# First expert weights of a routed feed-forward block: scaled beforehand by ScalarE and fetched per tile by DMA, in place of a VectorE pick per tile

## The reference

```python
def _ffn(xn, rw, W1, W2):
    ms = jnp.mean(xn * xn, axis=-1, keepdims=True)
    h = xn * jax.lax.rsqrt(ms + RMS_EPS) * rw          # rw: one weight per channel and expert
    return jax.nn.silu(h @ W1) @ W2                    # W1 128x256, W2 256x128
gates = jax.nn.softmax(xf @ router_w, axis=-1)
top_v, top_i = jax.lax.top_k(gates, TOP_K)             # 2 of 14
masked = jnp.zeros_like(gates).at[jnp.arange(N)[:, None], top_i].set(top_v)
masked = masked / (masked.sum(axis=-1, keepdims=True) + EPS)
routed = jax.vmap(lambda rw_, W1_, W2_: _ffn(xf, rw_, W1_, W2_))(rms_w, w1, w2)
routed_out = jnp.einsum('end,ne->nd', routed, masked)
shared = jax.vmap(lambda rw_, W1_, W2_: _ffn(xf, rw_, W1_, W2_))(rms_w_s, w1_s, w2_s).sum(0)
x = _layernorm(x + routed_out + shared)                # x: the mixer's normalised output
```

## Time and profile before

| | |
|---|---|
| runs | 769.55 us median of 3 (768.49 to 770.16) |
| span of the profiled execution | 769.2 us; the page gives no other time for it |
| busy share of the span | TensorE 85%, VectorE 77%, GpSimd 65%, ScalarE 58% |
| instructions of VectorE | 1744, of them 141 picks |
| DMA | 70.8 MB, mean 92 GB/s |

### The profile page before, as it was taken

How to read it: one execution, slowest core, us unless ns; L and a number is a source line. 1 busy time by engine, 2 the same in 40 slices (tenths; PEclk the granted TensorE clock), 3 DMA queues, 4 the chain that set the end, 5 groups by cost and what they waited for, 6 DMA issues and landing times.

```text
span 769.2 us, 14716 instructions
## 1 busy us (share of the span) xinstructions
PE 651.3 (85%) x4299; PEld 554.7 (72%) x4299; DVE 596.1 (77%) x1744; ACT 444.7 (58%) x1225; POOL 501.3 (65%) x545
## 2 busy tenths in 40 slices
PE   5987798999999999999999997965988878767830
PEld 4765576788888888888888886854987768656720
DVE  4999999999999999999999864427447343698875
ACT  4885688867877876787787543411223111346445
POOL 1144565887797897888888776556655656566561
PEclk9999999999999999999999998878889889997865
DMA  8541111211221121111111055114222236536126
GB/s 305 193 138 42 43 43 41 64 57 55 62 64 62 60 62 50 63 64 60 59 50 62 22 167 192 45 55 101 80 80 77 76 80 172 168 100 205 60 80 218
DMA packets 62638, 70.76 MB, mean 92 GB/s; under 512 B 10335, under 2 KB 45285, under 8 KB 62304
## 3 DMA queue, kind: packets, MB, share of 16 engines
q1 hardware_dynamic: 41568, 47.70, 19.6%
q0 software_dynamic: 8608, 16.87, 6.5%
q10 hardware_dynamic: 12384, 5.26, 2.9%
HBM read 48.55 MB, written 23.01 MB: 93 GB/s over the span
## 4 chain that ended last, share of the span: by engine, by line
PE 60%; DVE 13%; issue 12%; ACT 7%; another core or an unknown queue 4%; ACTq 2%; DMA 1%; DVEq 0%; SPq 0%
PE bank L745 7%; PE bank L817 6%; PE bank L826 6%; PE bank L884 6%; PE bank L770 5%; PE bank L800 5%; DVE xbcT_area L1155 3%; PE bank L881 3%; PE bank L871 3%; PE bank L833 3%; PE bank L785 3%; PE bank L888 2%; DVE decay_area L1163 2%; ACT x L933 2%
## 5 line engine op out<-in xcount | busy, mean ns | idle before, releaser
L623 POOL DMA_INDIRECT returned<-xT,slots_in x141 | 142.1, 1008 | 107.6 <-DVE xT L1453 67.3
L669 POOL DMA_INDIRECT dispatched<-rows,row_u x128 | 143.7, 1123 | 33.9 <-issue 31.8
L745 PE MATMUL bank<-xT 128*128 128x128 f32 x564 | 92.0, 316 | 43.4 <-issue 24.9
L1155 DVE SCALAR_TENSOR_TENSOR xbcT_area<-raw,conv_w,xbcT_area 128x512 f32<-128x512 f32 x162 | 123.9, 766 | 2.9 <-ACT xbcT_area L999 2.9
L745 PEld LDWEIGHTS bank<-xT 128*128 128x128 f32 x564 | 82.7, 226 | 50.7 <-issue 42.4
L944 ACT ACTIVATE raw<-bank 128x512 f32<-128x512 f32 (+1 forms) x71 | 39.8, 590 | 126.9 <-remote 61.5
L661 POOL TENSOR_TENSOR state_kept<-state,whole 128x256 f32<-128x256 f32 x56 | 72.1, 1288 | 59.0 <-DVE state L1181 49.1
L1453 DVE COPY xT<-bank 128x512 f32<-128x512 f32 (+1 forms) x36 | 24.3, 676 | 90.5 <-remote 72.8
L770 PE MATMUL bank<-xbcT_area,raw 128*128 x564 | 83.4, 308 | 4.7 <-issue 4.6
L1163 DVE TENSOR_TENSOR_SCAN decay_area<-decay_area,ident_heads 128x512 f32<-128x512 f32 x64 | 85.0, 1329 | 0.0
L770 PEld LDWEIGHTS bank<-xbcT_area,raw 128*128 128x128 f32 x564 | 79.6, 224 | 7.0 <-issue 7.0
(11 more groups left out here) (228 smaller groups left out, 1497.0 us busy)
## 6 DMA issues: line engine op xcount, KB each, us to landing
decay_area<-decay_rows SPq DMA_DIRECT2D x64, 256.0 KB
slots_in<-dispatched ACTq DMA_DIRECT2D x77, 64.5 KB
hid<-returned SPq DMA_DIRECT2D x18, 256.0 KB
slots_in<-dispatched SPq DMA_DIRECT2D x64, 64.5 KB
xT<-xT_dram SPq DMA_DIRECT2D x8, 512.0 KB, 7.9
x<-x_dram SPq DMA_DIRECT2D x8, 512.0 KB, 7.8
out_dram<-x SPq DMA_DIRECT2D x16, 256.0 KB
xT<-returned SPq DMA_DIRECT2D x14, 256.0 KB
```

The costliest lines, as they stand in the source:

```text
L623: e.indirect_dma_start(returned, bass.IndirectOffsetOnAxis(ap=slots_in[sb_][:, n, D:ROW].bitcast(U32), axis=0), slots_out[b][:, n * P:(n + ...
L669: e.indirect_dma_start(dispatched, bass.IndirectOffsetOnAxis(ap=row_u[t % 2][:, m:m + 1], axis=0), rows[t % 3][:, k, c4, :], None).then_in ...
L745: mm = e.matmul(bank[:, off:off + P], w1_now[b][:, k * P:(k + 1) * P], slotsT[gr % len(slotsT)][:, n % 4 * P:(n % 4 + 1) * P], start=True, ...
L1155: e.scalar_tensor_tensor(o, r[:, n:n + W], conv_w[:, k, TAPS - 1 - n:TAPS - n], o, ALU.mult, ALU.add).then_inc(S["conv"])
```

## The change

- The 14 routed experts' first weights have an SBUF area of their own (`w1_area`, 14 KB in a partition). SyncE loads them there in step 22 of the mixer; ScalarE multiplies each expert's 128x256 by its norm weights in steps 24 to 37, in place, one in each step; SyncE waits for the 14 and writes the 1792 KB to a DRAM tensor `w1_ready` in step 40.
- SyncE's queue fetches for each tile its expert's 128x256 (128 KB) from `w1_ready`, with the expert's number from a register, into a ring of 3 groups of 4 (`w1_ring`, in the area of the mixer's decays). The fetch for group gr waits until the first matmuls of group gr-3 are done. It stands behind the slot load of the same group and ahead of `pick`.
- VectorE's picks, their register loads and the 8 buffers are gone; TensorE's first matmuls wait for the fetch and read the ring.
- SyncE's `pick` stands one group nearer (`PICKS_BEHIND = 6` in place of the 7 of the slot buffers), and 11 of the picks are in the loop over groups, not 10.
- The 14 KB come in part from `dynamic_dma_scratch_size=2048`: the area in each partition that holds the descriptors of GpSimd's DMAs is 2048 bytes, not the usual 16384.

```diff
     ROUTED_AT = [NC + 2, *range(NC + 3, NC + 13, 2), *range(NC + 13, LAST)]
+    W1_FROM = 24
+    PICKS_BEHIND = 6
...
+    w1_ready = nc.dram_tensor("w1_ready", [P, NR, HB * P], F32, kind="Internal").ap()
...
-        w1_routed = decay_area[:].rearrange("p n h i -> p (n h i)")[:, 0:NR * HB * P].rearrange("p (e f) -> p e f", e=NR)
+        w1_area = sb("w1_area", [P, NR * HB * P])
+        w1_routed = w1_area[:].rearrange("p (e f) -> p e f", e=NR)
+        w1_ring = decay_area[:].rearrange("p n h i -> p (n h i)")[:, 0:3 * 4 * HB * P].rearrange("p (b n f) -> p b n f", b=3, n=4)
...
+                if c == W1_FROM - 2:
+                    e.dma_start(w1_routed, w1_v[:, 0:NR]).then_inc(S["w1r_loaded"], 16)
+                if c == W1_FROM + NR + 2:
+                    on.wait_ge("w1r_scaled", NR)
+                    e.dma_start(w1_ready, w1_routed).then_inc(S["w1r_stored"], 16)
...
+            def fetch_w1(gr, experts):
+
+                b = gr % 3
+                if gr >= 3:
+                    on.wait_ge("routed_hidden", 2 * (gr - 3) + 2)
+                for n in range(len(slot_tiles(gr))):
+                    e.dma_start(w1_ring[:, b, n, :], w1_ready[:, bass.ds(experts[4 * (gr % 2) + n], 1), :].rearrange("p o f -> p (o f)")).then_inc(S[f"w1_in{b}"], 16)
+
-            picks_beside = min(NM, GROUPS - len(slots_in) - LAST_A)
+            picks_beside = min(NM, GROUPS - PICKS_BEHIND - LAST_A)
...
-                if gr == 1:
-                    on.wait_ge("mix", NC)
-                    e.dma_start(w1_routed, w1_v[:, 0:NR]).then_inc(S["w1r_loaded"], 16)
+                if gr == 0:
+                    on.wait_ge("w1r_stored", 16)
...
                     load_slots(e, gr, first_rows)
-
-                m = gr - len(slots_in) - LAST_A
+                if gr == 0:
+                    on.wait_ge("mix", NC)
+                if gr % 2 == 0:
+                    w1_experts = experts_of(on, ET.SP, gr)
+                fetch_w1(gr, w1_experts)
+
+                m = gr - PICKS_BEHIND - LAST_A
...
-                    on.wait_ge("w1_picked", n + 1)
+                    gr = n // 4
+                    on.wait_ge(f"w1_in{gr % 3}", 16 * tiles_upto(gr, 3))
...
-                        mm = e.matmul(bank[:, off:off + P], w1_now[b][:, k * P:(k + 1) * P], slotsT[gr % len(slotsT)][:, n % 4 * P:(n % 4 + 1) * P], start=True, stop=True)
+                        mm = e.matmul(bank[:, off:off + P], w1_ring[:, gr % 3, n % 4, k * P:(k + 1) * P], slotsT[gr % len(slotsT)][:, n % 4 * P:(n % 4 + 1) * P], start=True, stop=True)
...
+                if at(i, W1_FROM, NR):
+                    n = i - W1_FROM
+                    on.wait_ge("w1r_loaded", 16)
+                    on.wait_ge("rms_w_loaded", 16)
+                    e.activation(w1_routed[:, n, :], w1_routed[:, n, :], ACT.Copy, scale=rms_w[:, n:n + 1]).then_inc(S["w1r_scaled"])
...
-            def pick_w1(gr):
-                if gr % 2 == 0:
-                    experts[:] = experts_of(on, ET.DVE, gr)
-                on.wait_ge("w1r_loaded", 16)
-                for n in slot_tiles(gr):
-                    was = n - len(w1_now)
-                    if was >= 0:
-                        on.wait_ge("routed_hidden", was // 2 + 1)
-                    e.tensor_scalar(w1_now[n % len(w1_now)], w1_routed[:, bass.ds(experts[n % 8], 1), :].rearrange("p o f -> p (o f)"), rms_w[:, bass.ds(experts[n % 8], 1)], None, ALU.mult).then_inc(S["w1_picked"])
...
-    nc = bacc.Bacc("TRN2", target_bir_lowering=False, num_devices=1)
+    nc = bacc.Bacc("TRN2", target_bir_lowering=False, num_devices=1, dynamic_dma_scratch_size=2048)
```

More of the change, by code:

```diff
@@ L33 @@
     "mix", "y_carried", "y_sum", "skip_diag", "gated", "residual", "ln_stats", "shift",
-    "logits", "top", "hot", "rows_taken", "shared_added", "w1_scaled", "early_total", "early_table", "table", "slots_turned", "w1_picked",
+    "logits", "top", "hot", "rows_taken", "shared_added", "w1_scaled", "early_total", "early_table", "table", "slots_turned",
     "routed_out", "gate", "routed_added", "last_rstd",
     "rate", "dt_exp", "chunk_decays", "step_decay", "rows_copied", "xbc_raw", "xbc_silu", "z_silu", "xdt", "g_squares", "bt",
-    "gT_copied", "x1", "x2", "xn", "xnT_copied", "hidden_silu", "routed_silu", "gate_exp", "second_scaled",
+    "w1r_scaled", "gT_copied", "x1", "x2", "xn", "xnT_copied", "hidden_silu", "routed_silu", "gate_exp", "second_scaled",
     "dt_raw", "chunk_sums", "rows_turned", "xbc", "z", "token_major", "gram", "state_add", "y_out", "gT",
@@ L342, in mamba_moe @@
         slotsT = [carve(W) for _ in range(3)]
-        w1_now = [carve(HB * P) for _ in range(8)]
         gexp = carve(NC * NR).rearrange("p (c r) -> p c r", c=NC)
@@ L394, in mamba_moe @@
             [f"{n}_loaded" for n, _, _ in small_params] + [f"xT{b}_loaded" for b in range(NB)]
-            + [f"x{b}_loaded" for b in range(NB)] + ["w_in_loaded", "w1_loaded", "w2_loaded", "w1r_loaded", "w2r_loaded",
+            + [f"x{b}_loaded" for b in range(NB)] + ["w_in_loaded", "w1_loaded", "w2_loaded", "w1r_loaded", "w1r_stored", "w2r_loaded",
                "filler_region", "filled", "dispatched0", "dispatched1", "stored", "decay_rows"]
@@ L398, in mamba_moe @@
             + [f"slots_in{b}" for b in range(len(slots_in))] + [f"returned{b}" for b in range(len(slots_out))]
-            + [f"picked{b}" for b in range(len(picked))])
+            + [f"w1_in{b}" for b in range(3)] + [f"picked{b}" for b in range(len(picked))])
         S = {n: ctx.enter_context(nc.semaphore(n)) for n in (*COMPUTE_SEMAPHORES, *dma_semaphores)}
@@ L739, in routed_hidden @@
                 for n in range(2 * n2, min(2 * n2 + 2, SLOT_TILES)):
-                    gr, b = n // 4, n % len(w1_now)
-                    on.wait_ge("w1_picked", n + 1)
+                    gr = n // 4
+                    on.wait_ge(f"w1_in{gr % 3}", 16 * tiles_upto(gr, 3))
                     on.wait_ge("slots_turned", gr + 1)
@@ L1442, in next_group @@
                     turned(gr + 2)
-                    pick_w1(gr + 2)
             def routed_group(gr):
@@ L1609, in vector_program @@
                         turned(gr)
-                        pick_w1(gr)
                 elif n is not None and n >= 2:
```

1 line of the change is left out of this document (removed).

## The result

| | runs | median us | range |
|---|---|---|---|
| before | 7 | 769.89 | 768.14 to 771.67 |
| changed | 7 | 774.75 | 772.21 to 778.20 |

The ratio is 1.0062 (95% interval 1.0039 to 1.0086): 0.6% slower. I had forecast 766.6 us, faster. The value lies in the range of 755 to 780 us, the sign is wrong.

A forecast was written before the change was run, and what follows sets the result against it. Bound: in the middle GpSimd's scatters plus a slow stretch (TensorE gaps, VectorE idle until just after the scatters), in the last part VectorE. Span 769.2 -3.1 -1.8 +1 +1 = 766.3, median 0.35 above: 766.6 us; range 755 to 780.

The forecast's parts named there:

- (c): Beginning of the routed part: without eight picks GpSimd's wait for row numbers goes, 1.8 us gained, bounds 0 and 4.
- (e): SyncE's queue in series: fills behind group 9's fetch delay group 10's transpose, 1 us lost, bounds 0 and 6.
- (a): Last part without VectorE's picks: slow stretches return and GpSimd becomes the limit, 3.1 us gained, bounds 13.2 or nothing.
- (b): Middle without VectorE's picks: they lie beside scatters and don't hold GpSimd up, 0, at most 5.6 us gained.
- the rival of the gain taken back: Slow stretches return and slow VectorE's small token steps, last part gains 0, beginning offset by fills: 769 us, chance 0.17.
- VectorE set free: Rival: in the last part no slow stretches return, a pair takes 11.3 us: 756.5 us in all, chance 0.12.
- (d): ScalarE's 14 scalings in the mixer: 0.38 us each, hidden while it idles for TensorE, 0; 5.3 us without that cover.
- (f): SyncE's token-row picks spread behind fetches: fit with 1.5 us to spare, 0; otherwise 1 us for each of 14 units.
- (g): Extra DMA traffic of 18 MB over 290 us: 1 us lost, bounds 0 to 1.8.
- the 32 us that the prediction gives beside its sum: Estimate from the skill's HBM latency rule for added traffic: up to 1.8 us per pair, not used in the sum.
- (h): Smaller descriptor area for GpSimd's scatters: two in flight, so 0; 36 us if each scatter waits for room.

The follow-up runs named there:

- no_picks_2: Kernel before without VectorE's picks, first matmuls reading fixed unscaled weights in place, with slow stretches: 765.63 us, ratio 1.0016.
- set 3: Set of runs with slow stretches; the changed kernel run again there took 769.34 us, ratio 1.0039 to the kernel before.
- pause_and_fills: Changed kernel with eight unread VectorE multiplications ahead of the row numbers and the fills ahead of group 9's fetch, with slow stretches: 765.41 us, ratio 0.9989.
- unread: Kernel before, picks kept, with 2048-byte area, 141 fetches nobody reads, fills ahead, token-row picks six groups behind; with slow stretches: 774.62 us, ratio 1.0125.
- near_rows: Kernel before with only SyncE's picks of token rows six groups behind in place of seven, with slow stretches: 764.91 us, ratio 0.9984.
- set 2: Set of runs without slow stretches; the changed kernel run again there took 715.30 us, ratio 0.9957 to the kernel before.
- no_picks: Kernel before without VectorE's picks, first matmuls reading fixed unscaled weights in place, without slow stretches: 715.05 us, ratio 0.9938.
- area_only: Kernel before with only GpSimd's descriptor area at 2048 bytes, without slow stretches: 717.22 us, ratio 0.998.
- behind_7: Changed kernel with SyncE's picks of token rows seven groups behind in place of six, with slow stretches: 787.23 us, ratio 1.0239.
- fills_ahead_3: Changed kernel with the fourteen fills moved ahead of group 9's fetch, with slow stretches: 768.51 us, ratio 1.0019.
- picks_on_act: Kernel before with its 141 picks given to ScalarE in place of VectorE, no fetches, with slow stretches: 775.28 us, ratio 1.0142.
- scalings_only: Kernel before with 2048-byte area plus the mixer's weight load, fourteen ScalarE scalings and store, results unread, with slow stretches: 765.26 us, ratio 0.997.
- pause_kept_2: Changed kernel with eight unread VectorE multiplications put back ahead of the row numbers, with slow stretches: 766.43 us, ratio 1.0028.

## Why the prediction was wrong

The step that failed is (c): I counted the pause ahead of the row numbers as 1.8 us to gain, and it was what kept a step of TensorE out of the slow stretch. With it (e) was mis-sized. With slow stretches the picks' end alone, (a), (b) and (c) together, was forecast at 4.9 us gained; `no_picks_2` measured 1.0016 (0.9996 to 1.0036), nothing. In substance that is the rival of the gain taken back, which I had at 0.17.

- **(a) picks, last part: right in size, in part by luck.** Forecast 3.1 us gained, with slow stretches returning; traced 4.8 for the same piece (75.39 to 70.61), and 3.6 in set 3 between scatters. The pairs of the changed kernel's last part are 13.1 to 13.9 us, and `no_picks_2` shows the round of 13.0 us that I took from the middle. But the stretches returned only in part: the changed kernel's copies wait 6.2 us in four such waits there, and `pause_and_fills` has 1.5 us in one and still needs 71.2 us. Nor is all of it the picks': `unread` keeps them and needs 72.4 us, and `near_rows` needs 74.6. In the runs without slow stretches the other bound nearly came true: in the profile of the changed kernel in set 2 the 11 groups take 64.9 us, 11.8 for a pair (groups 31 to 33: 672.62 to 684.05, 11.4), with 11.3 forecast for VectorE set free. How much of that is the picks is open: `no_picks` needs 70.0 us there and `area_only` 71.3.
- **(b) picks, middle: right**, 0. The scatters' mean is 1005 ns for 1008. The rule that VectorE's two-port instructions hold GpSimd up (the Trainium skill, "SBUF — State Buffer", Who interferes with whom) doesn't show in these scatters.
- **(c) beginning: wrong.** Forecast 1.8 gained. The wait went, and 0.2 us were lost to group 4. All twelve profiles with slow stretches split by the pause, whatever else their kernels have:

  | | TensorE idle before the router step that the changed kernel has at 481.11, us | 97th scatter to group 4, us |
  |---|---|---|
  | no pause: changed, changed in set 3, `behind_7`, `fills_ahead_3`, `no_picks_2`, `picks_on_act` | 6.35, 3.38, 7.91, 7.91, 7.85, 4.20 | 87.4, 86.1, 88.6, 88.8, 88.6, 90.0 |
  | pause: before, `near_rows`, `scalings_only`, `pause_kept_2`, `pause_and_fills`, `unread` | none shown in any | 87.2, 84.2, 83.4, 84.5, 82.2, 89.2 |

  `unread` is late for the reason given with it. The kernel before is 3 to 4 us over its near relatives in this stage, in an execution that was slow among its runs, and that hid the loss in the first comparison. `pause_and_fills` (0.9989, up to 1.0007) against `fills_ahead_3` (1.0019, from 0.9997), from two sets, prices it at 0.3%, some 2 us; the intervals just overlap.
- **(d) scalings: right in sum.** They took 0.565 us each, not 0.38, and the mixer is 0.9 us later besides the piece at the lower clock; but `scalings_only` is no slower than before.
- **(e) SyncE in series: right in place, mis-sized.** Fills from 545.53 (543.8 forecast), 14.0 us (7 to 16), transposes at 564.42 (up to 8 late; 8.0). I took 1 us, near the quick end, since I thought the fills would miss the slow stretch. The two profiles of the changed kernel with slow stretches lose 1.6 and 1.7 us between groups 4 and 12; the fills moved ahead give 2.4 us in set 2 and 0.8 in set 3, so 1 to 2.4 for my 1. The pause and the fills have in common that I priced a wait of the trace and not what stands beside a run of scatters.
- **(f) spread picks of rows: right.** They arrive; `behind_7` shows that there was no group to spare.
- **(g) traffic: not decided.** A pair of the middle is as long as before (598.36 to 611.56, 13.2 us, in a stretch with a DMA share of 0.59), so slow stretches are not longer. There are 17 remote waits for 14, but that says nothing of the fetches: `scalings_only`, which has none, has 17 too, and the changed kernel in set 3 has 15. In the middle one run has four scatters in place of eight, and takes 7.2 us with its wait for one group, which is most of the middle's 2.2 us (timeline of POOL, changed kernel):

```profile
632.68 0.97 POOL L644 DMA_INDIRECT returned<-xT,slots_in  x1 [3.22 <-DVE xT L1466]
...
639.87 0.97 POOL L644 DMA_INDIRECT returned<-xT,slots_in  x1 [2.38 <-DVE xT L1466]
```

  `unread` costs over 1%, but 4.8 us of it lie where the fetches meet the load that the changed kernel doesn't have; what the fetches alone cost in the changed kernel no run shows. My 1 us stays possible. Nothing of the size of the 32 us that the prediction gives beside its sum shows.
- **(h) the area: right**, no loss.

The mark of 766.6 had an error of its own: I set the median 0.35 us over the span. A run is 1.7 to 1.9 us longer than its span in every run since; the profiled execution of before was slow among its runs.

The sign goes with the slow stretches: 0.9957 without, 1.0039 and 1.0062 with them. With them the freed VectorE brings no time (`no_picks_2`), since what the last part gains the start loses, and the pause and the fills together make the difference between 0.4 to 0.6% slower and level (`pause_and_fills`). That the stretches themselves turn the sign, and nothing else about those chips, is argued and not shown: every set has one kind only. Open stays what makes a slow stretch, and whether the chip or something else about those runs brings it; and 3.6 us of the 4.9, which no trace of the first runs holds.

## What to carry to other kernels

Before removing work from an engine, ask whether the round goes over it at all: eight scatters, the stretch behind them and one copy made the round of the middle here, and no pick. A wait can be a shield: the 2 us for which GpSimd waited kept a whole step of TensorE ahead of a stall. A queue written in one line is paid where most is queued behind a new wait; moving fourteen small DMAs ahead of one fetch gave 2.4 us, as much again as the whole change, where there are no slow stretches. And an experiment that adds the new part without taking the old one out prices both at once: `unread` carried two weight transfers at the start of the routed part, where either kernel has one.

## What the runs showed of the hardware

- The same program took 718 and 719 us in two sets and 765 to 767 us in three (769.89 us in the first runs), over 6% apart, by set and chip. All of it lies in the routed part. There VectorE's copies wait 67 to 102 us in all in stretches that end some 1.6 to 1.9 us behind the last of a run of GpSimd's indirect DMAs; two of the four chips had none. The scatters themselves take 0.97 us in both.
- A pause of 0.9 to 4.6 us in such a run of indirect DMAs moved the stretch: TensorE had no idle time before one step in six profiles with the pause, and 3.38 to 7.91 us in six without.
- GpSimd's descriptor area at 2048 bytes, in place of the usual size, was no slower: 0.998 (0.9964 to 0.9996), and 0.997 (0.995 to 0.999) together with the scalings.
- TensorE's clock fell to the lower level for 3.4 us in the busy mixer (0.50 granted, TensorE at work throughout) in the profile of the changed kernel, which is 1.7 us of work at the higher one; the other profiles show none to two such pieces there, near 77, 85 or 121 us, and kernels of both kinds have them.
